# Moving four linear products, one bias addition and one bias row in a one-core recommendation-tower kernel

## The reference, cut to what matters

```python
e = stack([tbl_n[ids[:, n]] for n in range(26)])          # 512 samples x 26 features x 64
x = layer_norm(dense @ Wd.T, gd, bd)                      # 512 x 128
y = layer_norm(einsum('bnd,ed->bne', e, Ws), gs, bs)      # 26 rows of 128 per sample
y = einsum('bne,pn->bep', y, Wsi)                         # mixed to 32 rows
T = concat([x, layer_norm(y, gsi, bsi)])                  # 33 rows of 128
Z = (T @ T.T)[lower triangle]                             # 528 numbers
z = layer_norm(Z @ Wl.T, gl, bl)[:384]                    # "linear"
h = relu(concat([z, dense]) @ W_top1 + b_top1)            # 512
h = relu(h @ W_top2 + b_top2)                             # 256
y = h @ W_top3                                            # 512 x 1, all in float32
```

## Time and profile before

| what | value |
|---|---|
| median of 3 runs (lowest, highest) | 170.69 us (170.27, 171.25) |
| the profiled execution: its own time | 172.12 us |
| its span, first to last instruction | 170.3 us |
| PE busy | 141.4 us (83%) |
| DVE busy | 130.5 us (77%) |
| POOL busy | 102.4 us (60%) |
| ACT busy | 98.5 us (58%) |
| PE clock granted | 1.0 of full speed |

### The profile page before, as it was taken

How to read it: one execution, slowest core, us unless ns; L and a number is a source line. 1 busy time by engine, 2 the same in 40 slices (tenths; PEclk the granted TensorE clock), 3 DMA queues, 4 the chain that set the end, 5 groups by cost and what they waited for, 6 DMA issues and landing times.

```text
span 170.3 us, 4661 instructions
## 1 busy us (share of the span) xinstructions
PE 141.4 (83%) x1819; PEld 105.9 (62%) x1819; DVE 130.5 (77%) x303; ACT 98.5 (58%) x245; POOL 102.4 (60%) x112
## 2 busy tenths in 40 slices
PE   0199876987796869896979998978899989999995
PEld 0084543634353557483967684948696848788994
DVE  6379769795949997898498995966899969784262
ACT  0303334888755868786488685744766767551140
POOL 3777777777777777777777777777777500021000
DMA  4923616142211113211111231111112300101000
GB/s 133 341 42 91 261 31 208 34 115 58 37 27 30 24 23 81 52 34 24 29 31 29 52 73 30 26 28 27 30 27 67 66 8 0 38 16 29 0 0 0
DMA packets 6009, 9.59 MB, mean 56 GB/s; under 512 B 2309, under 2 KB 3544, under 8 KB 5860
## 3 DMA queue, kind: packets, MB, share of 16 engines
q0 software_dynamic: 3424, 3.46, 11.1%
q1 hardware_dynamic: 2232, 5.08, 9.4%
q10 hardware_dynamic: 332, 0.76, 1.2%
HBM read 8.01 MB, written 0.00 MB: 47 GB/s over the span
## 4 chain that ended last, share of the span: by engine, by line
POOL 49%; PE 19%; issue 18%; DVE 8%; ACT 3%; DMA 3%; DVEq 0%; ACTq 0%
POOL g_sb L262 48%; PE psW L359 3%; PE psB L325 2%; PE psB L379 2%; DVE B L849 2%; DVE ssB L856 1%; DMA g_sb<-in_table,row_id 1%; PE psU L306 1%; PE psZ L431 1%; PE psG L291 1%; DMA ids_sb<-in_ids 1%; PE psZ L340 1%; PE psH L379 1%; DVE T L869 1%; PE psW L404 1%
## 5 line engine op out<-in xcount | busy, mean ns | idle before, releaser
L262 POOL DMA_INDIRECT g_sb<-in_table,row_id x104 | 100.4, 965 | 31.7 <-issue 31.4
L849 DVE TENSOR_TENSOR B<-psB,bias 128x512 f32<-128x512 f32 x31 | 20.0, 686 | 13.5 <-PE psB L325 12.5
L306 PE MATMUL psU<-wsi_x,g_sb 128*128 128x192 f32 (+4 forms) x128 | 21.2, 309 | 5.9 <-DVE g_sb L842 5.7
L306 PEld LDWEIGHTS psU<-wsi_x,g_sb 128*128 128x128 f32 x128 | 19.0, 190 | 11.0 <-DVE g_sb L842 11.0
L653 ACT ACTIVATE Zs<-psZ 32x264 f32<-32x264 f32 x59 | 22.3, 378 | 1.1
L625 ACT ACTIVATE sqB<-B 128x512 f32<-128x512 f32 x31 | 18.7, 629 | 6.7 <-DVE B L849 6.7
L869 DVE TENSOR_TENSOR T<-B,psG 128x512 f32<-128x512 f32 x31 | 21.3, 686 | 1.1
L856 DVE TENSOR_REDUCE ssB<-sqB 128x16 f32<-128x512 f32 x32 | 21.7, 677 | 0.1
L325 PE MATMUL psB<-U,ws_g 64*128 64x512 f32 x64 | 18.1, 641 | 3.9 <-ACT U L614 3.7
L291 PEld LDWEIGHTS psG<-gram,sT 128*128 128x128 f32 x104 | 12.8, 191 | 10.3 <-ACT sT L601 10.0
L291 PE MATMUL psG<-gram,sT 128*128 128x128 f32 x104 | 15.9, 291 | 0.7 <-ACT sT L601 0.7
(11 more groups left out here) (161 smaller groups left out, 220.7 us busy)
## 6 DMA issues: line engine op xcount, KB each, us to landing
g_sb<-in_table,row_id POOLq DMA_INDIRECT x104, 2.5
wl_sb<-in_wl SPq DMA_DIRECT2D x1, 1280.0 KB, 5.4
w_sb<-in_w SPq DMA_DIRECT2D x2, 512.0 KB, 4.4
w_sb<-in_w SPq DMA_DIRECT2D x1, 768.0 KB, 4.2
small_sb<-in_small SPq DMA_DIRECT2D x1, 615.5 KB, 4.0
dense_sb<-in_dense ACTq DMA_DIRECT2D x1, 512.0 KB, 6.2
Zt<-Zs SPq DMA_DIRECT2D x3, 80.0 KB
Zt<-Zs SPq DMA_DIRECT2D x3, 70.0 KB
```

The costliest lines, as they stand in the source:

```text
L262: pool.indirect_dma_start(g_sb[:, k, h * DSP:(h + 1) * DSP], None, table, bass.IndirectOffsetOnAxis(row_id[:, 2 * k + h:2 * k + h + 1], 0) ...
L306: mm = pe.matmul(psU[:, (lo - US * j) * PROJ:(hi - US * j) * PROJ], g_sb[:, SLOTS * b + c, :], wsi_x[:, c, lo - s0:hi - s0, :], start=(n = ...
L849: dve.tensor_tensor(B[:, h, :].rearrange("p (s j) -> p s j", j=PROJ), psB[h][:, :].rearrange("p (s j) -> p s j", j=PROJ), bias[:, :].rearr ...
```

## The change

Five edits.

1. `AHEAD`: products 0 to 3 of block 2's linear layer stand directly behind mix(14) on PE, ahead of transposes(15) and project(14); products 4 to 9 stay where the ten stood.
2. Unit 15's bias: the one-row product into `psB[0]` becomes two products of 64 rows (all but one of them zero), one into `psB[0]`, one into `psB[1]`; they wait for both halves of unit 14. DVE's `add_b(15, 1)` goes, and ACT's second square and DVE's `norm_b` read `psB[1]`.
3. The last layer's bias: relu(p + zsd*b) is written max(p, -zsd*b) + zsd*b. DVE makes `least` = -zsd*b (two instructions) and both maxima; the four passes of L457 and ACT's relu L812 go; the second part, zsd times the sum over w3*b, is one product of one row and one column into `psY`, between L468 and L473.
4. Last copies: ACT takes quarter 2 of unit 15 from DVE, and its `third_squares(1)` stands behind two copies of unit 14 instead of ahead of them.
5. At the start, `bs_sb` is loaded as 128 rows of 128 (64 KB in place of 1.5 KB), and the product for `wsum` is widened to all partitions, with two more products for the sum of w3*b.

```diff
-EARLY, ALL = (9, 9, 10), FLIN // P * CW
+AHEAD, EARLY, ALL = (0, 0, 4), (9, 9, 10), FLIN // P * CW
...
                 if last:
 
-                    pe.wait_ge(B_added, 2 * u - 1)
-                    pe.matmul(psB[0][:, :].rearrange("p (s j) -> p s j", j=PROJ), bs_sb[0:1, 0:E],
-                              wsum[:, :].rearrange("p (o j) -> p o j", o=1).broadcast_to([1, US, PROJ]),
-                              start=True, stop=False)
+                    pe.wait_ge(B_added, 2 * u)
+                    for h in range(2):
+                        hs = slice(h * DSP, (h + 1) * DSP)
+                        pe.matmul(psB[h][:, :].rearrange("p (s j) -> p s j", j=PROJ), bs_sb[hs, :],
+                                  wsum[hs, 0:PROJ].rearrange("p (o j) -> p o j", o=1).broadcast_to([DSP, US, PROJ]),
+                                  start=True, stop=False)
...
-                for f in range(K2):
-                    pe.matmul(psO[f][:, 0:BS], bs_sb[0:1, E + f * P:E + (f + 1) * P], zsd[0:1, :], start=True,
-                              stop=False)
...
+                pe.matmul(psY[0:1, 0:BS], wsum[0:1, PROJ:PROJ + 1], zsd[0:1, :], start=True, stop=False)
                 for k in range(K2):
                     pe.wait_ge(h2T_f[k], 1)
                     mm = pe.matmul(psY[0:1, 0:BS], w3_c[:, k:k + 1], h2T_last[:, k * BS:(k + 1) * BS],
-                                   start=(k == 0), stop=(k == K2 - 1))
+                                   start=False, stop=(k == K2 - 1))
...
                 mix(t)
+                if late and j == 0:
+                    linear(b, 0, AHEAD[b])
                 if t + 1 < UNITS and not behind(t + 1):
                     transposes(t + 1)
                 project(t)
...
-                    linear(b, 0, EARLY[b])
+                    linear(b, AHEAD[b], EARLY[b])
...
                     keep_z(t - 1, 0)
                     deviation_b(t, 1)
-                    third_squares(1)
                     keep_z(t - 1, 1)
                     keep_z(t - 1, 2)
+                    third_squares(1)
...
-            act.wait_ge(h2_f, 1)
-            act.activation(h2T_last[:, 0:BS], psO[0][:, 0:BS], ACT.Relu).then_inc(h2T_f[0], 1)
...
+                for f in range(K2):
+                    dve.tensor_scalar(least[:, f, :], zsd[:, :], b2_c[:, f:f + 1], -1.0, ALU.mult,
+                                      ALU.mult).then_inc(least_ready, 1)
                 dve.reciprocal(part[:, :], zsd[0:1, :]).then_inc(W_recip, 1)
-                dve.wait_ge(h2_f, 2)
-                dve.tensor_scalar(h2T_last[:, BS:2 * BS], psO[1][:, 0:BS], 0.0, None, ALU.max).then_inc(h2T_f[1], 1)
+                for f in range(K2):
+                    dve.wait_ge(least_ready, f + 1)
+                    dve.wait_ge(h2_f, f + 1)
+                    dve.tensor_tensor(h2T_last[:, f * BS:(f + 1) * BS], psO[f][:, 0:BS], least[:, f, :],
+                                      ALU.max).then_inc(h2T_f[f], 1)
...
                 if t < UNITS - 1:
                     add_b(t, 0)
-                add_b(t, 1)
+                    add_b(t, 1)
```

More of the change, by code:

```diff
@@ L112, in tower @@
         wsi_x = sb("wsi_x", [P, SLOTS, SPAN, PROJ])
-        wsum = sb("wsum", [1, PROJ])
+        wsum = sb("wsum", [P, PROJ + 1])
+        least = sb("least", [P, K2, BS])
         bias = sb("bias", [P, PROJ])
@@ L325, in project @@
                     pe.matmul(psB[h][:, :], ws_g[h * DSP:(h + 1) * DSP, :], U[h * DSP:(h + 1) * DSP, u % 2, :],
-                              start=not (last and h == 0), stop=True).then_inc(B_done, 1)
+                              start=not last, stop=True).then_inc(B_done, 1)
             def inner(u):
@@ L346, in linear @@
             def linear(b, lo, hi):
+                if lo == hi:
+                    return
                 if lo == 0:
@@ L353, in linear @@
                         pe.wait_ge(m_kept, 1)
-                elif b == LAST - 1:
+                elif b == LAST - 1 and hi == ALL:
                     pe.wait_ge(y_copied, b)
@@ L462, in last_block @@
                         mm = pe.matmul(psO[f][:, 0:BS], w2_sb[:, k, f * P:(f + 1) * P],
-                                       h1T_last[:, k * BS:(k + 1) * BS], start=False, stop=(k == K1 - 1))
+                                       h1T_last[:, k * BS:(k + 1) * BS], start=(k == 0), stop=(k == K1 - 1))
                         if k == K1 - 1:
@@ L531, in _ @@
             pe.wait_ge(w_prep, 5)
-            pe.matmul(psU[0:1, 0:PROJ], sel_sb, wsi_c[:, 0, :], start=True, stop=True).then_inc(wsum_done, 1)
+            pe.matmul(psU[:, 0:PROJ], sel_sb.broadcast_to([P, P]), wsi_c[:, 0, :], start=True, stop=True)
+            for k in range(K2):
+                mm = pe.matmul(psU[:, PROJ:PROJ + 1], w3_c[:, k:k + 1].broadcast_to([P, P]), b2_c[:, k:k + 1],
+                               start=(k == 0), stop=(k == K2 - 1))
+            mm.then_inc(wsum_done, 1)
             dense_part(0)
@@ L536, in _ @@
             pe.wait_ge(wsum_ready, 1)
-            pe.matmul(psU[:, 0:PROJ], bs_sb[:, 0:E], wsum[:, :], start=True, stop=True).then_inc(bias_done, 1)
+            pe.matmul(psU[:, 0:PROJ], bs_sb[0:DSP, :], wsum[0:DSP, 0:PROJ], start=True, stop=True).then_inc(bias_done, 1)
             transposes(0)
@@ L616, in squares_b @@
             def squares_b(u, h):
-                if u == UNITS - 1 and h == 0:
-                    act.wait_ge(B_done, 2 * u + 1)
-                    at = psB[0][:, :]
+                if u == UNITS - 1:
+                    act.wait_ge(B_done, 2 * u + h + 1)
+                    at = psB[h][:, :]
                 else:
-                    act.wait_ge(B_added, min(2 * u + h + 1, 2 * UNITS - 1))
+                    act.wait_ge(B_added, 2 * u + h + 1)
                     at = B[:, h, :]
@@ L788, in _ @@
                 step(t)
-            keep_z(UNITS - 1, 0)
-            keep_z(UNITS - 1, 1)
+            for gq in range(3):
+                keep_z(UNITS - 1, gq)
             deviation_w(LAST - 1)
@@ L867, in norm_b @@
                     dve.wait_ge(Z_done, 4 * (u - 1))
-                at, r = (psB[0][:, :], rB_last[:, :]) if u == UNITS - 1 and h == 0 else (B[:, h, :], rB[:, h, :])
+                at, r = (psB[h][:, :], rB_last[:, h, :]) if u == UNITS - 1 else (B[:, h, :], rB[:, h, :])
                 dve.tensor_tensor(T[:, u % 2, h, :, 2:], at.rearrange("p (s j) -> p s j", j=PROJ),
@@ L1094, in _ @@
             third_zT(1)
-            for u, gq in ((UNITS - 2, 3), (UNITS - 1, 2), (UNITS - 1, 3)):
+            for u, gq in ((UNITS - 2, 3), (UNITS - 1, 3)):
                 dve.wait_ge(Z_done, 4 * u + gq + 1)
@@ L1158 @@
     ws2 = np.concatenate([x["L0_rec_Ws"].T, x["L0_rec_Ws"].T])
+    bs_rows = np.zeros((P, E), np.float32)
+    for h in range(2):
+        bs_rows[h * DSP] = x["L0_rec_bs"]
     arrays = {
```

14 lines of the change are left out of this document (7 added, 7 removed).

## The result

The changed kernel took 173.23 us (median of 7; 172.02 to 175.35), the kernel before, measured beside it, 171.25 (median of 7; 170.27 to 172.55). The ratio is 1.0101, 95% interval 1.0065 to 1.0137: 1.7 us slower, where 0.67 had been forecast. The ratio leaves out one of its seven executions, the one of 175.35 us, which fell in a slower state of the chip. Its profiled execution took 173.23 us with a span of 171.4.

A forecast was written before the change was run, and what follows sets the result against it. Gathers bound the kernel to about 114 us, then a chain of compute; +0.60 - 0.15 + 0.22 = +0.67 us on a base of 170.69 gave 171.36 us, range 170.4 to 172.0.

The forecast's parts named there:

- What bounds the kernel: Whole kernel: POOL's gathers to about 114 us, compute behind; earlier edits cost nothing unless large, later chain edits count fully.
- At the start, a few passes and 62 KB more lie ahead of unit 0 ... 0: Start of the kernel: the added passes and load fall in the stretch that the gathers bound, cost 0.
- Edit 1: PE behind mix(14): four products wait for relu2, project(14) +0.79, net +0.60 us, range 0.4 to 0.8.
- the hold by linear: PE ahead of mix(15): block 2's ten products no longer hold it, which gives back 0.2 us.
- the hole is really free: Rival, PE behind mix(14): h2_ready is there already, project(14) keeps its place; sum -0.1, 170.6 us; chance 0.18.
- The relays ... took 2.0 to 2.6 us, so about 136.1: earlier: Other wait of the four products behind mix(14): relays land about 136.1 us, ahead of relu2's end at 136.85.
- Edit 2: Unit 15's biases: DVE's addition goes, second square ends 0.17 earlier; -0.15 us, bounds -0.17 and 0.
- So PE's time is unchanged: PE at unit 15's biases: the new pair takes about project's 1.06 us, the one-row product took 1.05.
- the bias pair doesn't overlap: Rival, unit 15's biases on PE: halves run one after the other, 2.1 us; +1.05, 172.4 us; chance 0.11.
- Edit 3: Last layer's bias: L457 hidden, maxima covered, new one-row product adds two passes; +0.22 us, bounds 0 and 0.3.
- all that is removed counts: Rival: L457 (-0.44) and the addition (0.69) were on the path, project(14) not delayed; -1.1, 169.6 us; chance 0.08.
- Edit 4: Last copies and block 2's later square: nothing won, as PE is busy, and variance not delayed; 0.

The follow-up runs named there:

- relu2_early: The changed kernel with ACT's relu2 of block 1 one unit earlier in the program, ahead of the last copy of unit 12; ratio to before 1.0104.
- no_ahead: The changed kernel without the four linear products of block 2 behind mix(14), all else as changed; ratio to before 1.0035.
- two_rows: The changed kernel with unit 15's bias pair as products of one row each in place of 64, loaded as two single rows; ratio to before 1.0096.
- old_tail: The changed kernel with the last layer's bias as it was before, its row loaded by a DMA of its own; ratio to before 1.0059.
- y_bias_early: The changed kernel with the psY product of the last bias moved ahead of the second layer's own products in the last block; ratio to before 1.0056.
- mended_lean: The kernel called mended, but w3*b2 is multiplied on DVE and summed by PE in the gap, without two start products; ratio to before 0.9982.
- mended: The changed kernel without products ahead and with the psY product ahead of layer 2; ratio to before 1.0014, and 1.0028 when run again.
- start_only: The kernel before with the new start alone (64 KB load, widened wsum product, two w3*b2 products), its results not used at the end; ratio to before 1.0025.

## Why the prediction was wrong, step by step

**What bounds the kernel.** Right behind 114 us: what shifts mix(15), the variance or the tail is found again at the last y. Two terms of the sum behind it were mis-sized, and the runs show by what: edit 1 cost +0.92 and not +0.60, edit 3 +0.44 and not +0.22; edit 2, better than forecast, took back 0.26 of these 0.54. A third failed step lies ahead of it: "So edits ahead of 114 us cost nothing unless they are large", and with it "At the start, a few passes and 62 KB more lie ahead of unit 0 ... 0". The few passes take 0.4 us in line on PE, and the kernels that have them measure 0.5 us more in the mean; how the one leads to the other, or whether it does, stays open.

**Edit 1**, +0.60 forecast, +0.92 measured. The mechanism was as told: PE idle behind mix(14), DVE's idle time up by 0.99, mix(15) waiting for DVE, and the hold by linear giving a little back. The rival "the hole is really free" fell. Three sizes were off: the first load runs 0.12 behind relu2's end and not 0.05; the transposes with what follows take 138.52 - 137.99 = 0.53 and not 0.36, of which 0.17 is issue; and the end of the hold gives back not 0.2 but 0.08. The last is a wrong choice between two rows: the prediction had 0.70 as its bound "if mix(15) is counted from the weight load at 142.70" and took 0.6 "as the matmul row is the one that U follows". U follows the load: it starts 144.16 - 142.70 = 1.46 us behind it before and 145.20 - 143.75 = 1.45 in the changed kernel, while from the matmul record it is 1.35 and 1.45. With the load counted, the forecast's 0.70 and the 0.21 that project(14) came later than forecast (1.54 against 1.33) make 0.91. "The relays ... took 2.0 to 2.6 us, so about 136.1: earlier" was wrong: 3.2 us in relu2_early, and in the changed kernel 3.4 at most. It did not change the sum, because relu2 ended then too, but it hid a second wait.

**Edit 2**, -0.15 forecast, -0.41 measured. DVE's part was right in kind, and near in size (-0.17 forecast, -0.21 measured): without `add_b` the two squares run back to back, and from project(15) to the variance no_ahead takes 5.43 us, before 5.74; 0.10 of this is project itself. "So PE's time is unchanged" failed: the pair takes 0.96 us in place of the one-row product's 1.05, and project behind it 0.96 in place of 1.06, because project's first weight load runs under the pair; two_rows, whose one-row pair takes 1.06 and leaves project at 1.06, loses 0.20 at the last y. The rival "the bias pair doesn't overlap" fell. Edit 2 was never run without edit 4, so the -0.41 is that of both.

The prediction put 0.065 us beside this edit, from what the Trainium skill ("Perfetto Trace Analysis", Optimizing Scalar/DVE Operations) states on DVE accesses to PSUM. The second norm_b of the changed kernel takes the 0.69 us that it took before:

```profile
150.10 0.69 DVE L876 TENSOR_TENSOR T<-psB,rB_last 128x512 f32<-128x512 f32 x1
```

That is no test of the page. The form of before read `B` from SBUF but its reciprocals from PSUM (`psG` in the earlier trace rows), so one operand lay in PSUM in both, and no run here has the form with none.

**Edit 3**, +0.22 forecast, +0.44 measured. L457 was hidden, the maxima were covered, the product is in line: right. Its length was not: "two passes" were priced at 0.11 each, but this product has one row and one column between products of 128 rows, and shows 0.40 between the outputs. Its own records are no longer than its neighbours'; the time lies between them. Before, the first weight load of the output of block 3 ran 0.11 ahead of its first matmul at 167.74, under the product ahead of it:

```profile
167.63 0.41 PEld L473 LDWEIGHTS psG<-h2T_last,small_sb 128*1 128x1 f32 x4
```

In the changed kernel the first load of the one-row product and that of the product behind it each follow 0.22 us without a load, and start with their own matmuls (168.53 and 168.53, 168.83 and 168.84). This fits two passes at their forecast 0.22 and 0.18 for the two loads that no longer run under a neighbour. The rival "all that is removed counts" fell: project(14) was delayed, and old_tail, with the four passes of L457, ends no later than y_bias_early without them.

**Edit 4**: 0 agrees with the sum of the parts, +0.95, against +0.97 for the whole; it was not run alone.

**The sum.** The forecast's +0.67 stands against +0.97 that the traces show and 1.7 (1.1 to 2.3) timed. With the 0.5 that kernels with the products measure on top it is 1.5. The rest, 0.2, is inside the interval. The time in us missed by 1.87, 173.23 against 171.36; 0.56 of this is the base, which was taken from three runs: 170.69, where seven gave 171.25 and 126 others medians of 171.2 to 171.4.

**A better version.** Without linear products ahead, with the bias pair and the psY product in the gap, the trace behind relu2 is 0.42 us shorter than before's. mended_lean, which also spares the two products at the start, measured 0.9982 (0.9961 to 1.0002), mended, with the start's products, 1.0014 and 1.0028: the best is mended_lean, and it is not clearly faster than before.

## What to carry to other kernels

An idle stretch on an in-order engine takes only work whose operands are there when it begins: list all the waits of what is moved in, each with its landing, because mending the later one uncovers the next. A tiny product costs by where it stands: in an idle stretch nothing, between two wide ones 0.40 us here. When a matmul's start is a term of a sum, take it from its first weight load, which can run under the product ahead of it: here the choice of row was worth 0.11 us, and a load that ran under its neighbour won 0.20 at the bias pair. Do not put work at the start down as free on the word of a chain that shows gathers there; time it alone, often enough to see half a microsecond. And take a forecast's base from many runs, not three.

## What the runs showed that was not expected

- Relays: seven transfers issued by SP at 0.64 to 0.86 us each landed 3.2 us after the last issue, where POOL's three took 2.0 to 2.6.
- A float32 product of one row and one column between products of 128 rows took 0.40 us of PE's row for its two passes; two passes of one row and 128 columns (L457), in a place of their own, had taken 0.21.
- Project, four passes of 64 rows in the two halves of the array, takes 1.06 us behind a one-row product and 0.96 behind a product of its own form, whose passes cover its first weight load.
- PE's granted clock fell somewhere from 70 to 76 us in 5 of 12 profiles of kernels with the products at the start, in none of 6 without; that against none in six does not tell that they cause it. In the changed kernel (columns: stretch, length, busy PE, PEld, DVE, ACT, POOL, granted clock, DMA share, GB/s):

```profile
68.00:70.00 2.00, 1.40 (x10) 1.21 (x10) 1.93 (x6) 1.74 (x6) 1.60 (x2) 1.00 0.46 111
70.00:72.00 2.00, 1.15 (x7) 0.52 (x7) 1.57 (x5) 0.79 (x3) 1.39 (x3) 0.89 0.14 26
72.00:74.00 2.00, 2.00 (x5) 0.50 (x6) 0.08 (x1) 1.88 (x3) 1.70 (x2) 0.50 0.18 32
74.00:76.00 2.00, 2.00 (x69) 1.78 (x70) 1.84 (x4) 1.35 (x3) 1.39 (x3) 0.75 0.09 17
```

PE had been idle for 1.45 us of the four ahead of 72 us, 0.78 of it waiting for a gather, and then project's four passes took 2.08 us at the 1.2 GHz level instead of 1.13 at 2.4 GHz:

```profile
71.46 0.42 PE L279 MATMUL psT<-small_sb,g_sb 128*128 128x128 f32 x1 [0.78 <-DMA g_sb<-in_table,row_id]
71.81 2.08 PE L328 MATMUL psB<-U,ws_g 64*128 64x512 f32 x4
```

In the kernel before PE was idle there for 0.83 us and kept its clock (1.00). But start_only was idle for 1.49 us of the same four and kept it too. Before, and then start_only:

```profile
68.00:70.00 2.00, 1.73 (x14) 1.54 (x13) 1.93 (x6) 1.74 (x6) 1.39 (x3) 1.00 0.42 84
70.00:72.00 2.00, 1.44 (x10) 0.69 (x8) 1.63 (x5) 1.28 (x4) 1.64 (x2) 1.00 0.20 33
```

```profile
68.00:70.00 2.00, 1.18 (x8) 1.08 (x8) 1.93 (x6) 1.74 (x6) 1.67 (x2) 1.00 0.45 103
70.00:72.00 2.00, 1.33 (x8) 0.73 (x8) 1.69 (x5) 1.06 (x3) 1.41 (x2) 1.00 0.12 25
```

So what makes an execution fall there is not shown. It may be part of the half microsecond ahead of relu2's end: that end stands at 136.90 us in the mean of the five profiles with the fall, at 136.39 in the seven others with the products and at 136.16 in the six without. This rival was not tested.
